# Three edits in two stages of a four-layer kernel: where the products of an attention layer are summed, where its sigmoid is written, and the place of one matrix product in a Fourier layer

## The chip, the cores and the metric

The kernel runs on one core of a Trainium2 chip. The time is the device time of one execution in microseconds (us), and lower is better. A NeuronCore has engines that run side by side, each with its own queue in program order: TensorE (PE, matrix products), VectorE (DVE), ScalarE (ACT), GpSimd (POOL, called Pool below) and the queues that issue DMAs (SP). They wait for each other by semaphores: a count that one engine raises and another waits for. SBUF is the on-chip memory of 128 partitions; PSUM is the small memory that TensorE writes its results to, which DVE and ACT can read and write too.

## The reference, cut to what matters

Four layers follow each other on an image of 2 x 64 channels (128 rows of the chip, one for each batch and channel) with 256 x 256 = 65,536 points; each adds its result to its input. The change touches the first and the third.

```python
# layer 0: attention over the nine neighbours of a point, two apart
un_em = _unfold3x3(em)
feature_score = jnp.einsum('bckhw,bchw->bkhw', un_em, em)
un_fea = _unfold3x3(inp)
comp_score = jax.nn.sigmoid(jnp.einsum('bckhw,c->bkhw', un_fea, w_comp))
phi = comp_score * feature_score
weighted_fea = jnp.einsum('bckhw,bkhw->bchw', un_fea, phi)
...
# layer 2: widen 64 channels to 384, filter 8 x 8 patches in frequency, 3 x 3 convolution, gate, project to 64
x = jnp.einsum('bchw,oc->bohw', x, w_in)
xf = jnp.fft.rfft2(xp) * fft_filter
xp = jnp.fft.irfft2(xf, s=(p, p))
x = lax.conv_general_dilated(x, w_dw, window_strides=(1, 1), padding=[(1, 1), (1, 1)], feature_group_count=C)
x1, x2 = jnp.split(x, 2, axis=1)
x = jax.nn.gelu(x1, approximate=False) * x2
return jnp.einsum('bchw,oc->bohw', x, w_out)
```

Before each layer the input is normalised by groups of channels. Layer 1 (two Mamba scans) and layer 3 (a cosine transform) are not touched.

## The kernel before

The stages run one after the other with a barrier between them: statistics and score maps, attention, Mamba, Fourier, cosine transform. In each stage every engine has its own program, and the order of the work is the order in which these programs are written; nothing is reordered by a planner.

**Attention** (`attention_layer`, from L366). The points are cut into 64 tiles of T = 1024 columns, and a step handles one tile; one short step more closes the stage, so there are 65. For tile s, TensorE multiplies the raw input `x` by a channel weight into `p_s` (`score`, L528: two halves of 512 columns). ACT takes the sigmoid of `p_s` into the SBUF buffer `sig` (L582), DVE forms `g` = (x - mean) * sig (`make_g`, L623) into a buffer with a margin, and ACT copies the margin from the tile before (L577). The nine neighbours are nine shifted reads of `g`: for k = 0 to 8 TensorE spreads the feature score of neighbour k to all channels in `p_f` (two PSUM buffers in turn, one bf16 product of two halves), and DVE multiplies it by the shifted `g` into `apr[k]` (L657). These nine products are summed in two places. Pool adds pairs of them in SBUF (L678, the list `PAIRS`: 0+1, 2+3, 4+5, 6+7, and 8 onto 6), and TensorE adds the four results into the PSUM tile `p_a` by products with the identity (`add`, in fp32; `SUMMED` tells how many of Pool's additions must be done). DVE then writes the output from `p_a` and the residual `xr` (`output`, L632) and takes its statistics (L645).

The order on TensorE in a step is: p_f 0, 1, 2, then the last addition of the step before (`add(s.other(-1), 6)`), p_f 3, 4, 5, the score of the next tile, p_f 6, add 0, p_f 7, add 2, p_f 8, add 4. All helpers run through `halves`, so every product of the stage has line L519. DVE's order is: products 0 to 4, output of the step before, products 5 and 6, its statistics, product 7, `make_g` of the next tile, product 8. With two p_f buffers, p_f k waits for product k-2.

**Fourier** (`fft_layer`, from L1378). A row r of 8 image lines is worked on in two slots, b = 0 and b = 1, one for each batch, 64 slots in all. In a slot TensorE runs through 24 ticks j (`slot`). The steps of the slot's own half: `conv` (one or two taps of the convolution as products into `p_c`, L1619), one at j = 1, 5, 9 and so on; these come first in a tick. `project` (L1627, L1629) multiplies the gated result of the slot before by the output weights, at j = 1 and j = 4. For the slot to come: `widen` (L1593) spreads a piece of the input over 384 channels into the single PSUM tile `p_fr`, at each odd j from 1 to 15; DVE multiplies it by the filter into `v` (`filter_`, L1853); `from_freq` (L1602) turns it back into `p_i` from j = 3 on, and ACT places it into `zb` (L1725). In slots b = 0 TensorE also turns the next row into frequencies (`turn`, L1572, and `to_freq`, L1582). Since `p_fr` is single, `widen` 1 waits until DVE has filtered `widen` 0's result.

DVE's program in a slot is 30 taps of the convolution (L1847, six units of five), with the filter for piece 0 after three taps, piece 1 after five, piece 2 after eight and so on (`FILTER_N`), and the additions of the residual (L1869) and the statistics (L1883) of the slot before at four places near the start. Pool adds ACT's taps (L1947) and multiplies for the gate (L1952, L1956).

Of the kernel before, what the change touches and what calls it, by code (L numbers as in the profile page):

```python
# [365 lines left out]
def attention_layer(nc, dram, fs, bn0, bn1, L, W, T):  # L366
# [11 lines left out]
    with ExitStack() as ctx:  # L378
        def sb(name, shape, dt=FP32):
            return ctx.enter_context(nc.sbuf_tensor(name, shape, dt))  # L380
# [11 lines left out]
        s_bias = sb("s_bias", [128, 1])  # L392
        x = [sb(f"ax{i}", [128, T]) for i in range(2)]
        xr = [sb(f"axr{i}", [128, T]) for i in range(2)]
        sig = [sb(f"sig{i}", [128, T]) for i in range(2)]
        g = [sb(f"g{i}", [128, GW]) for i in range(2)]
        fb = [sb(f"fb{i}", [96, T], BF16) for i in range(2)]
        pr = [sb(f"apr{i}", [128, T]) for i in range(NKS)]
# [24 lines left out]
        gnorm = GroupNorm(nc, ctx, "a", bn0, pair, p_a)  # L423
        block = ctx.enter_context(nc.Block())

        PAIRS = [(0, 1), (2, 3), (4, 5), (6, 7), (6, 8)]
        SUMMED = {0: 1, 2: 2, 4: 3, 6: 5}

        class Step:

# [83 lines left out]
        @block.tensor  # L514
        def _(pe):
            def halves(out, w, rhs, start=True, stop=True):
                for i in range(2):
                    c = slice(i * HALF, (i + 1) * HALF)
                    last = nc.tensor.matmul(out[:, c], w, rhs[:, c], start=start, stop=stop)  # L519
                return last  # L520

            pe.wait_ge(w_in, 48)
            gnorm.pe(pe)
            pe.wait_ge(gnorm.done, 1)
            nc.tensor.matmul(p_s[:, 0:1], comp[:, :], gnorm.gn[:, 6:7], start=True, stop=True).then_inc(bias_ps, 1)
            pe.wait_ge(ready, 1)

            def score(s):  # L528
                pe.wait_ge(x_in[s.par], s.pair * 16 + 16)
                if s.from_(1):  # L530
                    pe.wait_ge(sig_done, s.nth(0, 1) - 1)
                halves(p_s, comp_s[:, :], x[s.par]).then_inc(s_ps, 1)

            def add(s, k):
                pe.wait_ge(paired, s.nth(SUMMED[k] - 1, len(PAIRS)))
                if k == 0 and s.from_(1):
                    pe.wait_ge(xo_done, s.nth(0, 1) - 1)
                halves(p_a, ident, pr[k], start=(k == 0), stop=(k == 6)).then_inc(acc_done, 1)

            def step(s):  # L540
                pe.wait_ge(f_in[s.par], s.pair * 48 + 48)
                for k in range(NKS):
                    if s.from_(1) or k >= 2:
                        pe.wait_ge(prod_done, s.nth(k, NKS) - 2)
                    halves(p_f[(s.par + k) % 2], fsel[:, k, :], fb[s.par]).then_inc(f_ps, 1)
                    if k == 2 and s.from_(1):
                        add(s.other(-1), 6)
                    if k == 5 and not s.last and not s.other(1).last:
                        score(s.other(1))
                    if k >= 6:  # L550
                        add(s, 2 * (k - 6))

            score(Step(0, 0))
            run(step)(pe)
            add(Step(0, NK), 6)

        @block.scalar
        def _(act):
            act.wait_ge(w_in, 48)
            gnorm.act(act)  # L560
            act.wait_ge(ready, 1)

            def load_maps(s):
                if s.from_(2):
                    act.wait_ge(f_ps, s.nth(-1, NKS) - NKS)
                width = PAD if s.last else T
                for part in range(3):
                    act.dma_start(fb[s.par][32 * part:32 * part + 2 * NKS, 0:width],
                                  fs[part, :, bass.ds(s.at(T), width)]).then_inc(f_in[s.par], 16)

            def prepare(s):

                if s.from_(1):
                    act.wait_ge(g_done, s.nth(0, 1) - 1)
                    if s.from_(2):
                        act.wait_ge(prod_done, s.nth(-1, NKS) - NKS)
                    nc.scalar.activation(g[s.par][:, 0:2 * PAD], g[1 - s.par][:, T:T + 2 * PAD], ACT.Copy).then_inc(carried, 1)  # L577
                if not s.last:
                    act.wait_ge(s_ps, s.nth(0, 1))
                    if s.from_(2):  # L580
                        act.wait_ge(g_done, s.nth(0, 1) - 2)
                    nc.scalar.activation(sig[s.par][:, :], p_s[:, :], ACT.Sigmoid, bias=s_bias[:, :]).then_inc(sig_done, 1)  # L582

            def step(s):
                if not s.last:
                    load_maps(s.other(1))
                    prepare(s.other(1))

            load_maps(Step(0, 0))
            prepare(Step(0, 0))  # L590
            run(step)(act)

        @block.vector
        def _(dve):
# [20 lines left out]
            def make_g(s):  # L615
                if s.last:
                    dve.wait_ge(carried, NK)
                    nc.vector.memset(g[s.par][:, 2 * PAD:GW], 0.0).then_inc(g_done, 1)
                    return
                dve.wait_ge(sig_done, s.nth(0, 1))  # L620
                if s.from_(2):
                    dve.wait_ge(carried, s.nth(0, 1) - 1)
                nc.vector.scalar_tensor_tensor(out=g[s.par][:, 2 * PAD:GW], in0=x[s.par][:, :], scalar=mean_n[:, :],  # L623
                                               in1=sig[s.par][:, :], op0=ALU.add, op1=ALU.mult).then_inc(g_done, 1)

            def output(s):
                dve.wait_ge(acc_done, s.nth(3, 4))
                dve.wait_ge(xr_in[s.par], s.pair * 16 + 16)
                if s.from_(2):
                    dve.wait_ge(x_out[s.par], s.pair * 16)  # L630
                    dve.wait_ge(bn_done, s.nth(0, 1) - 1)
                nc.vector.scalar_tensor_tensor(out=xo[s.par][:, :], in0=p_a[:, :], scalar=rstd, in1=xr[s.par][:, :],  # L632
                                               op0=ALU.mult, op1=ALU.add).then_inc(xo_done, 1)
# [14 lines left out]
            def step(s):  # L648
                dve.wait_ge(g_done, s.nth(0, 1))
                if s.from_(1):  # L650
                    dve.wait_ge(carried, s.nth(0, 1) - 1)
                for k in range(NKS):
                    at = PAD + OFFS[k]
                    dve.wait_ge(f_ps, s.nth(k, NKS))
                    if s.from_(1) and k % 2 == 0 and k < 8:
                        dve.wait_ge(acc_done, s.nth(k // 2, 4) - 4)
                    nc.vector.tensor_tensor(out=pr[k][:, :], in0=g[s.par][:, at:at + T], in1=p_f[(s.par + k) % 2][:, :],  # L657
                                            op=ALU.mult).then_inc(prod_done, 1)
                    if k == OUT_K and s.from_(1):
                        output(s.other(-1))  # L660
                    if k == STAT_K and s.from_(1):
                        statistics(s.other(-1))
                    if k == G_K and not s.last:
                        make_g(s.other(1))
# [6 lines left out]
        @block.gpsimd  # L671
        def _(pool):
            def step(s):
                for n, (a, z) in enumerate(PAIRS):
                    pool.wait_ge(prod_done, s.nth(z, NKS))
                    if n == 4:
                        pool.wait_ge(paired, s.nth(3, 5))
                    nc.gpsimd.tensor_tensor(out=pr[a][:, :], in0=pr[a][:, :], in1=pr[z][:, :], op=ALU.add).then_inc(paired, 1)  # L678

            run(step)(pool)  # L680
# [697 lines left out]
def fft_layer(nc, dram, bn2, bn3, H, W):  # L1378
# [22 lines left out]
    with ExitStack() as ctx:  # L1401
# [158 lines left out]
        def _(pe):  # L1560
# [91 lines left out]
            def slot(r, b, s, first=False, no_next=False, no_row=False):  # L1652
                nb, ns = 1 - b, s + 1
                rows_left = not (isinstance(r, int) and r == NR - 1)
                for j in range(TICKS):
                    if j in CONV_AT:
                        conv(s, b, CONV_AT[j])
                    if not first and j in PROJECT_AT:
                        project(s - 1, nb, r if rows_left else None, PROJECT_AT.index(j))
                    if not no_next:  # L1660
                        if j in WIDEN_AT:
                            widen(ns, r + b, nb, WIDEN_AT[j])
                        if j in BACK_AT:
                            from_freq(ns, BACK_AT[j])
                        if j == NEXT_AT:
                            conv(ns, nb, 0)
                    if b == 0 and not no_row:
                        if j in TURN_AT:
                            turn(r + 1, TURN_AT[j])
                        if j in FREQ_AT:  # L1670
                            to_freq(r + 1, FREQ_AT[j])
# [665 lines left out]
```

## Time and profile before

| | us |
|---|---|
| runs of the kernel before, median of 3 | 20574.27 |
| lowest and highest of them | 20570.39, 20582.24 |
| the profiled execution, its own time | 20572.38 |
| its span | 20570.6 |
| attention stage, about | 1157 |
| Fourier stage, about | 3490 |

The profile comes from one execution. Its span is 1.8 us shorter than that execution's own time, and its time is 1.9 us below the median. TensorE's granted clock was 0.772 of full speed on average over the whole kernel: 0.89 in the attention stage and 0.96 in the Fourier stage. In a timeline row the first two numbers are the start and the time until the end of the row's last instruction, and the last bracket is the idle time of the engine ahead of it with the instruction that ended it.

### The profile page before, as it was taken

The numbers are of one execution on the slowest core, as the hardware profiler recorded it, in microseconds if no ns is written. First come the engines' busy times: TensorE is split into PE (matmuls) and PEld (weight loads), VectorE is DVE, ScalarE is ACT, GpSimd is POOL, SyncE is SP. The second block draws the span as 40 slices with busy tenths as digits, with TensorE's granted clock in tenths as the row PEclk, the third lists the DMA queues.
The fourth block names the chain that finished last, engine by engine and source line by source line (L and its number), as shares of the span: only waits on it lengthen the run. The fifth ranks groups of instructions, "written<-read, shape, count | busy, mean of one in ns | idle before, by whom it ended". The sixth has DMA issues, their size and how long they took to land. (4 is left out here: it accounts for less than half of the span.)

```text
span 20570.6 us, 184019 instructions
## 1 busy us (share of the span) xinstructions
PE 13872.1 (67%) x47074; PEld 5005.0 (24%) x47074; DVE 18437.9 (90%) x11898; ACT 11403.8 (55%) x12716; POOL 17177.7 (84%) x7352
## 2 busy tenths in 40 slices
PE   4885666666666666666666666666666668888885
PEld 2331111111111111111111111111111134444444
DVE  5778999999999999999999999999999979888896
ACT  1115555555555555555555555556555546666663
POOL 3777888888888888888888888888888868888891
PEclk8887777777777777777777777777777779999997
DMA  3224554555445554555445544555455511111113
GB/s 120 93 90 122 130 127 124 127 128 131 124 124 131 129 127 125 128 130 128 126 126 130 130 125 126 129 128 128 125 127 131 127 47 31 31 31 31 31 27 135
DMA packets 615483, 2240.63 MB, mean 109 GB/s; under 512 B 74881, under 2 KB 92147, under 8 KB 591091
## 3 DMA queue, kind: packets, MB, share of 16 engines
q1 hardware_dynamic: 610146, 2232.63, 42.0%
q10 hardware_dynamic: 5265, 7.14, 0.1%
q8 instruction: 33, 0.54, 0.0%
q14 instruction: 39, 0.32, 0.0%
HBM read 990.77 MB, written 174.96 MB: 57 GB/s over the span
## 5 line engine op out<-in xcount | busy, mean ns | idle before, releaser
L1358 POOL TENSOR_TENSOR h<-h,c_bc 128x1024 f32<-128x1024 f32 x4096 | 9597.4, 2358 | 1050.1 <-DVE h L1310 1036.5
L1310 DVE TENSOR_TENSOR_SCAN h<-da,state,px 128x1024 f32<-128x1024 f32 x3328 | 7810.9, 2347 | 524.0 <-PE py L1016 123.1
L1175 ACT ACTIVATE da<-d_bc,a_neg 128x1024 f32<-128x1024 f32 x3328 | 3811.8, 1145 | 3907.2 <-DVE h L1310 3882.4
L1002 PE MATMUL px<-cf,bsel 32*128 32x512 f32 x4096 | 2005.3, 1074 | 3605.7 <-DVE h L1310 3605.7
L1304 DVE TENSOR_TENSOR px<-px,du_bc 128x1024 f32<-128x1024 f32 x3328 | 4099.1, 1232 | 235.1 <-DMA du_bc<-du 46.2
L1947 POOL TENSOR_TENSOR acc<-acc,ta 128x1024 f32<-128x1024 f32 (+1 forms) x1040 | 2424.8, 2339 | 482.1 <-DVE acc L1847 344.0
L1016 PE MATMUL py<-h,ysel 128*32 128x512 f32 x16384 | 2370.4, 704 | 529.5 <-POOL h L1358 529.5
L1847 DVE SCALAR_TENSOR_TENSOR p_c<-zb,w_dw,p_c 128x1024 f32<-128x1024 f32 (+1 forms) x1560 | 1987.1, 1274 | 43.6 <-PE p_c L1619 11.1
L1310 DVE TENSOR_TENSOR_SCAN h<-px,state,xs 128x1024 f32<-128x1024 f32 x768 | 1772.7, 2338 | 274.6 <-ACT px L1175 272.3
L1350 POOL TENSOR_TENSOR xs<-du_bc,b_bc 128x1024 f32<-128x1024 f32 x768 | 1804.4, 2350 | 0.0
L1002 PEld LDWEIGHTS px<-cf,bsel 32*128 32x128 f32 x4096 | 488.6, 291 | 4714.0 <-DVE h L1310 4662.0
L1746 ACT ACTIVATE ta<-zb,w_dw 128x1024 f32<-128x1024 f32 (+1 forms) x1040 | 1169.0, 1129 | 317.2 <-POOL acc L1947 295.3
L1325 POOL TENSOR_TENSOR delta<-delta,sp 128x1024 f32<-128x1024 f32 x256 | 600.5, 2346 | 781.3 <-ACT sp L1127 781.3
L1602 PE MATMUL p_i<-basis,v 128*128 128x128 f32 x6144 | 967.2, 294 | 383.0 <-ACT zb L1725 373.1
L678 POOL TENSOR_TENSOR apr<-apr 128x1024 f32<-128x1024 f32 x325 | 824.1, 2543 | 383.0 <-DVE apr L657 377.5
L1619 PE MATMUL p_c<-zb,diag 128*128 128x512 f32 x2064 | 1007.4, 622 | 166.1 <-DVE acc L1847 131.3
L973 PE MATMUL pm<-hx,w_tap 128*128 128x512 f32 x1024 | 752.8, 902 | 534.5 <-ACT hx L1083 534.5
L1016 PEld LDWEIGHTS py<-h,ysel 128*32 128x32 f32 x16384 | 472.5, 121 | 2323.4 <-issue 1501.1
L944 PE MATMUL pm<-u,w_bc 128*64 128x512 f32 x1024 | 915.3, 1049 | 175.9 <-ACT sr L1099 175.9
L1602 PEld LDWEIGHTS p_i<-basis,v 128*128 128x128 f32 x6144 | 782.0, 194 | 812.8 <-ACT zb L1725 559.9
L657 DVE TENSOR_TENSOR apr<-g,p_f 128x1024 f32<-128x1024 f32 x585 | 690.3, 1215 | 253.5 <-PE p_f L519 252.1
L1725 ACT ACTIVATE zb<-p_i 128x384 f32<-128x384 f32 x1024 | 524.3, 512 | 633.0 <-PE p_i L1602 628.9
(222 smaller groups left out, 20340.6 us busy)
## 6 DMA issues: line engine op xcount, KB each, us to landing
d_bc<-delta SPq DMA_DIRECT2D x1024, 512.0 KB, 8.4
du_bc<-du SPq DMA_DIRECT2D x1024, 512.0 KB, 8.7
c_bc<-c_rows_dram SPq DMA_DIRECT2D x1024, 512.0 KB, 5.3
b_bc<-c_rows_dram SPq DMA_DIRECT2D x256, 512.0 KB, 8.0
hx<-x_dram SPq DMA_DIRECT2D x252, 256.5 KB, 6.0
st_x<-in_x_dram SPq DMA_DIRECT2D x32, 1024.0 KB, 4.9
ax<-in_x_dram SPq DMA_DIRECT2D x64, 512.0 KB, 3.4
xr<-x_dram SPq DMA_DIRECT2D x64, 512.0 KB, 5.9
```

The source lines that it names most:

```text
L1002: last = nc.tensor.matmul(px[(t.par + q + q // 2) % 2][:, cut], bsel[rows, q, :], cf[rows, cut], start=True, stop=True)
L1016: last = nc.tensor.matmul(py[32 * j:32 * j + 32, cut], ysel[:, :], h[:, (4 * q + j) % 8, cut], start=False, stop=(q == Q - 1))
L1175: nc.scalar.activation(out[:, :], d_bc[:, n % J, :], ACT.Exp, scale=a_neg[t.l][:, n:n + 1]).then_inc(da_done, 1)
L1304: nc.vector.tensor_tensor(out=x[:, :], in0=b[:, :], in1=du_bc[:, j, :], op=ALU.mult).then_inc(m1_done, 1)
L1310: nc.vector.tensor_tensor_scan(h[:, n % 8, PAD:T + PAD], a[:, :], x[:, :], state[:, 2 * t.l + t.b, n:n + 1], ALU.mult, ALU.add).then_inc(s ...
L1350: nc.gpsimd.tensor_tensor(out=xs[i][:, :], in0=du_bc[:, n % J, :], in1=b_bc[:, :], op=ALU.mult).then_inc(xs_done, 1)
L1358: nc.gpsimd.tensor_tensor(out=h[:, n % 8, 0:T], in0=h[:, n % 8, PAD:T + PAD], in1=c_bc[q % 2][:, :], op=ALU.mult).then_inc(m2_done, 1)
L1602: last = nc.tensor.matmul(p_i[:, c], v[j // 2 % 2][:, j % 2, c], basis[:, 1, :], start=True, stop=True)
L1619: last = nc.tensor.matmul(p_c[odd(s, u)][:, i * 512:i * 512 + rows * W], diag[:, oc, t, :], zb[b][:, oc, y:y + rows, dx:dx + W], start=(t ...
L1746: nc.scalar.activation(ta[odd(s, u)][t][:, 0:n * W].rearrange("p (y x) -> p y x", y=n), zb[b][:, oc, y:y + n, dx:dx + W], ACT.Identity, sc ...
L1847: nc.vector.scalar_tensor_tensor(out=out, in0=zb[b][:, oc, y:y + n, dx:dx + W], scalar=w_dw[:, oc, m:m + 1], in1=other, op0=ALU.mult, op1= ...
L1947: nc.gpsimd.tensor_tensor(out=acc[h][oc][:, c], in0=acc[h][oc][:, c], in1=ta[o][t][:, c], op=ALU.add).then_inc(added, 1)
```

## The change

In the attention stage Pool gets a sixth addition, 2 onto 0, third in its order, which waits for the second; TensorE's `add` of product pair 2 goes, so that three remain (0, 4 and 6). `add` 0 moves from behind p_f 6 to behind p_f 7 and waits for Pool's third addition; `add` 4 stays behind p_f 8 and waits for Pool's fourth. The counts that DVE waits for follow. The sigmoid is written over its own input in `p_s` and the two `sig` buffers go; `make_g` reads it from there, and `score` of the next tile waits until `make_g` has read it. In the Fourier stage `widen` stands ahead of `project` within a tick. The only tick that has both is j = 1, so only `widen` 0 and the first `project` of a slot change places.

```diff
-        sig = [sb(f"sig{i}", [128, T]) for i in range(2)]
...
-        PAIRS = [(0, 1), (2, 3), (4, 5), (6, 7), (6, 8)]
-        SUMMED = {0: 1, 2: 2, 4: 3, 6: 5}
+        PAIRS = [(0, 1), (2, 3), (0, 2), (4, 5), (6, 7), (6, 8)]
+        SUMMED = {0: 3, 4: 4, 6: 6}
+        NP, NA = len(PAIRS), len(SUMMED)
...
-                    pe.wait_ge(sig_done, s.nth(0, 1) - 1)
+                    pe.wait_ge(g_done, s.nth(0, 1) - 1)
...
-                    if k >= 6:
-                        add(s, 2 * (k - 6))
+                    if k == 7:
+                        add(s, 0)
+                    if k == 8:
+                        add(s, 4)
...
-                    if s.from_(2):
-                        act.wait_ge(g_done, s.nth(0, 1) - 2)
-                    nc.scalar.activation(sig[s.par][:, :], p_s[:, :], ACT.Sigmoid, bias=s_bias[:, :]).then_inc(sig_done, 1)
+                    nc.scalar.activation(p_s[:, :], p_s[:, :], ACT.Sigmoid, bias=s_bias[:, :]).then_inc(sig_done, 1)
...
-                                               in1=sig[s.par][:, :], op0=ALU.add, op1=ALU.mult).then_inc(g_done, 1)
+                                               in1=p_s[:, :], op0=ALU.add, op1=ALU.mult).then_inc(g_done, 1)
...
-                dve.wait_ge(acc_done, s.nth(3, 4))
+                dve.wait_ge(acc_done, s.nth(NA - 1, NA))
...
-                    if s.from_(1) and k % 2 == 0 and k < 8:
-                        dve.wait_ge(acc_done, s.nth(k // 2, 4) - 4)
+                    if s.from_(1) and k in SUMMED:
+                        dve.wait_ge(acc_done, s.nth(list(SUMMED).index(k), NA) - NA)
...
-                    if n == 4:
-                        pool.wait_ge(paired, s.nth(3, 5))
+                    if n in (2, NP - 1):
+                        pool.wait_ge(paired, s.nth(n - 1, NP))
...
+                    if not no_next and j in WIDEN_AT:
+                        widen(ns, r + b, nb, WIDEN_AT[j])
                     if not first and j in PROJECT_AT:
                         project(s - 1, nb, r if rows_left else None, PROJECT_AT.index(j))
                     if not no_next:
-                        if j in WIDEN_AT:
-                            widen(ns, r + b, nb, WIDEN_AT[j])
```

TensorE in the attention stage, one step from its p_f 5 on (`p_s` is the score of the next tile, `p_a<-apr0` is add 0). Before:

```order
L519 MATMUL p_f1<-fb0,fsel 128x512 x2
L519 MATMUL p_s<-ax1,comp_s 128x512 x2
L519 MATMUL p_f0<-fb0,fsel 128x512 x2
L519 MATMUL p_a<-apr0,a_mats 128x512 x2
L519 MATMUL p_f1<-fb0,fsel 128x512 x2
L519 MATMUL p_a<-apr2,a_mats 128x512 x2
L519 MATMUL p_f0<-fb0,fsel 128x512 x2
L519 MATMUL p_a<-apr4,a_mats 128x512 x2
```

The same stretch of TensorE after the change:

```order
L519 MATMUL p_f1<-fb0,fsel 128x512 x2
L519 MATMUL p_s<-ax1,comp_s 128x512 x2
L519 MATMUL p_f0<-fb0,fsel 128x512 x2
L519 MATMUL p_f1<-fb0,fsel 128x512 x2
L519 MATMUL p_a<-apr0,a_mats 128x512 x2
L519 MATMUL p_f0<-fb0,fsel 128x512 x2
L519 MATMUL p_a<-apr4,a_mats 128x512 x2
```

Add 0 has moved behind p_f 7 (the second `p_f1`), and the add of `apr2` is gone.

Pool in the attention stage, one whole step after the change (before, the third of these rows is not there):

```order
L678 TENSOR_TENSOR apr0<-apr0,apr1 128x1024 [waits product]
L678 TENSOR_TENSOR apr2<-apr2,apr3 128x1024 [waits product]
L678 TENSOR_TENSOR apr0<-apr0,apr2 128x1024 [waits products_paired,product]
L678 TENSOR_TENSOR apr4<-apr4,apr5 128x1024 [waits product]
L678 TENSOR_TENSOR apr6<-apr6,apr7 128x1024 [waits product]
L678 TENSOR_TENSOR apr6<-apr6,apr8 128x1024 [waits products_paired,product]
```

The new addition stands ahead of 4+5, 6+7 and 6+8, which all queue behind it.

TensorE in the Fourier stage, tick j = 1 of a slot, as one piece of the difference (`p_c` is conv, `p_qo<-ge` is project, `p_fr` is widen; ISA rows are waits):

```order
 L1619 MATMUL p_c1<-zb0,diag 128x512 x2
+L1588 ISA
+L1493 ISA
+L1593 MATMUL p_fr<-w_in,ft 128x384 x2
 L1641 ISA
 L1627 MATMUL p_qo<-ge00,w_out 64x512
...
 L1629 MATMUL p_qo<-ge11,w_out 64x512
-L1588 ISA
-L1493 ISA
-L1593 MATMUL p_fr<-w_in,ft 128x384 x2
```

Widen 0 stands directly behind conv now, and the four products of the first project follow it instead of leading it.

## Rows read from the trace of the kernel before

**Rows 1.** Busy time by stretch: start:end, length, then each engine; last granted clock, DMA.

```profile
392.00:1549.00 1157.00, 960.90 (x2454) 371.60 (x2454) 903.18 (x841) 138.16 (x127) 820.84 (x324) 0.89 0.28 92
16690.00:20180.00 3490.00, 2814.95 (x13806) 1505.57 (x13806) 3045.48 (x2731) 2142.26 (x2672) 3027.15 (x1300) 0.96 0.11 28
```

**Rows 2.** Waits in the attention stage: who for whom, us in total, times, longest.

```profile
DVE apr L657 <- PE p_f L519: 252.1, 144, 4.6
```

**Rows 3.** Timeline of DVE, one attention step at full clock (start, us, instructions).

```profile
913.73 2.35 DVE L657 TENSOR_TENSOR apr<-g,p_f 128x1024 f32<-128x1024 f32 x2 [3.76 <-PE p_f L519]
...
920.64 1.20 DVE L657 TENSOR_TENSOR apr<-g,p_f 128x1024 f32<-128x1024 f32 x1
921.76 1.28 DVE L623 SCALAR_TENSOR_TENSOR g<-ax,mean_n,sig 128x1024 f32<-128x1024 f32 x1
...
930.22 1.22 DVE L657 TENSOR_TENSOR apr<-g,p_f 128x1024 f32<-128x1024 f32 x1 [2.39 <-PE p_f L519]
```

**Rows 4.** Timeline of TensorE, the same step and the end of the one before.

```profile
909.87 3.38 PE L519 MATMUL p_a<-apr,a_mats 128*128 128x512 f32 x4 [1.51 <-POOL apr L678]
...
919.75 1.88 PE L519 MATMUL p_a<-apr,a_mats 128*128 128x512 f32 x4
921.47 0.60 PE L519 MATMUL p_f<-fb,fsel 96*128 96x512 bf16 x2
921.90 1.88 PE L519 MATMUL p_a<-apr,a_mats 128*128 128x512 f32 x4
...
927.76 1.98 PE L519 MATMUL p_a<-apr,a_mats 128*128 128x512 f32 x4 [1.54 <-POOL apr L678]
```

**Rows 5.** Timeline of Pool, the same step.

```profile
915.02 2.36 POOL L678 TENSOR_TENSOR apr<-apr 128x1024 f32<-128x1024 f32 x1 [2.91 <-DVE apr L657]
...
921.93 8.08 POOL L678 TENSOR_TENSOR apr<-apr 128x1024 f32<-128x1024 f32 x3 [1.08 <-DVE apr L657]
```

**Rows 6.** All instructions of two lines: count, min/median/max ns, first and last start.

```profile
L678 POOL TENSOR_TENSOR apr<-apr x325: 2331/2356/3350, 394.7 to 1550.0; 128x1024 f32<-128x1024 f32 x163
L623 DVE SCALAR_TENSOR_TENSOR g<-ax,mean_n,sig x64: 1277/1279/1284, 391.0 to 1511.7; 128x1024 f32<-128x1024 f32 x64
```

**Rows 7.** Waits in the Fourier stage, columns as in Rows 2.

```profile
DVE v L1853 <- PE p_fr L1593: 355.8, 256, 21.1
...
PE p_fr L1593 <- DVE v L1853: 73.7, 63, 2.3
...
POOL acc L1947 <- POOL ge L1956: 22.4, 93, 0.2
```

**Rows 8.** Timeline of TensorE around j = 1 of a slot b = 1.

```profile
18069.61 1.99 PE L1619 MATMUL p_c<-zb,diag 128*128 128x512 f32 x4
18071.52 1.08 PE L1627 MATMUL p_qo<-ge,w_out 128*64 128x512 f32 x4
...
18073.54 0.92 PE L1593 MATMUL p_fr<-w_in,ft 64*128 64x384 f32 x4
18075.61 0.92 PE L1593 MATMUL p_fr<-w_in,ft 64*128 64x384 f32 x4 [1.16 <-DVE v L1853]
```

**Rows 9.** Timeline of DVE in that slot: filter 0, the first residual addition, filter 2.

```profile
18074.60 0.96 DVE L1853 TENSOR_TENSOR v<-p_fr,filt 128x768 f32<-128x768 f32 x1 [1.26 <-PE p_fr L1593]
...
18076.66 0.68 DVE L1869 TENSOR_TENSOR fxo<-p_qo,fxr 128x512 f32<-128x512 f32 x1
...
18084.77 0.96 DVE L1853 TENSOR_TENSOR v<-p_fr,filt 128x768 f32<-128x768 f32 x1 [0.34 <-PE p_fr L1593]
```

**Rows 10.** Timeline of a slot b = 0: TensorE's conv at j = 1.

```profile
18011.57 3.78 PE L1619 MATMUL p_c<-zb,diag 128*128 128x512 f32 x4 [3.74 <-DVE acc L1847]
```

**Rows 11.** DVE's filter 0 of the same slot.

```profile
18019.14 0.96 DVE L1853 TENSOR_TENSOR v<-p_fr,filt 128x768 f32<-128x768 f32 x1 [3.78 <-PE p_fr L1593]
```

**Rows 12.** Timeline of Pool, late in that slot b = 1.

```profile
18105.03 4.88 POOL L1947 TENSOR_TENSOR acc<-acc,ta 128x1024 f32<-128x1024 f32 x2 [1.52 <-DVE acc L1847]
```

**Rows 13.** ACT's normalisation of a row in the Fourier stage: all of them.

```profile
L1707 ACT ACTIVATE hn<-raw,f_gn x31: 2077/2079/2082, 16751.5 to 19904.9; 128x2048 f32<-128x2048 f32 x31
```

## The prediction, as it was put on record

> **What bounds the kernel now.** I read the busy time by stretch first [rows 1]. The change lies in two of the stages. The attention stage takes about 1157 us of the span, the Fourier stage about 3490. In neither is an engine full: DVE, the busiest, works 903 of 1157 us and 3045 of 3490 us. So each stage is held by a chain that runs from engine to engine, and the question is which links of it the edits shorten. The views that show this are the waits and then the timelines.
>
> In the attention stage DVE loses 252.1 us, all of it to TensorE's p_f [rows 2]. The timeline of a step shows where. Product 3 starts at 913.73 and product 3 of the next step at 930.22: a step is 16.49 us here [rows 3]. Most of DVE's idle time is the 2.39 us ahead of product 3. That product needs p_f 3, which stands behind the last addition of the step before on TensorE, and this addition waited 1.54 us for Pool until 927.76 [rows 4]. Pool was late because its addition 6+7 can start only after product 7 (end 920.64 + 1.20 = 921.84, start 921.93), and 6+8 follows [rows 3, 5]. The loop is therefore: product 3, DVE's work up to product 7, Pool's 6+7 and 6+8, TensorE's add 6 and p_f 3, product 3.
>
> Two things lengthen it. First, Pool's three additions from 921.93 take 8.08 us, where a lone one takes 2.36; 8.08 - 2 x 2.36 = 3.36, which is the longest addition of the stage, 3.350 us against a median of 2.356 [rows 5, 6]. It is 6+7, and it starts while DVE's `make_g` runs (921.76 to 923.04). `make_g` is DVE's only operation in the step whose two large inputs both lie in SBUF; the addition that runs from 915.02 to 917.38 takes its normal 2.36 us beside products and the output, which read one input from PSUM [rows 3, 5]. Second, the clock: add 6 took 1.98 us at 927.76 and 3.38 us at 909.87, one at the level of 2.4 GHz and the other mostly at 1.2 GHz [rows 4]. The 64 `make_g` run from 391.0 to 1511.7 us, so a mean step is 1120.7 / 63 = 17.8 us, 1.3 us above the step at full clock [rows 6]. The granted clock of the stage is 0.89 [rows 1].
>
> In the Fourier stage DVE waits 355.8 us for p_fr [rows 7]. In a slot b = 1, TensorE runs conv (1.99 us), both parts of the first project (18071.52 to 18073.54) and only then widen 0 [rows 8]. DVE waited 1.26 us for it [rows 9]. And since p_fr is single, TensorE then stood idle 1.16 us until DVE had filtered it [rows 8]. That idle time comes once in nearly every slot: 73.7 us in 63 cases, 1.17 each [rows 7].
>
> **The change, part by part: attention.** I take the time from the start of product 3.
> (1) The sigmoid in PSUM. `make_g` now has one input in PSUM, like the output and the products, so I let 6+7 take its 2.36 us: 1.0 us less on the loop. ACT's sigmoid is not on the loop, and `make_g`'s own time (1.28 us) I leave. The new wait of the score for `make_g` costs nothing, since the products of the same `g` run before it in any case.
> (2) The sixth addition. Pool's first addition of the loop, 2+3, starts 915.02 - 913.73 = 1.29 us in [rows 3, 5]. Behind it come 0+2, 4+5, 6+7 and 6+8. Products 5 and 7 end at 4.7 and 8.1 us, before Pool gets to them, so the five run one behind another: 5 x 2.36 = 11.8 us, done at 13.1 us. Pool pays up to 0.24 us where it waits for its own result (22.4 / 93 in the Fourier stage [rows 7]), twice here: 13.1 to 13.6. The three additions of 8.08 us hold one such wait and no visible gap, so I take 13.2. Before, 6+8 ended at 921.93 + 8.08 - 2.36 = 927.65, that is 13.92 us in. Pool's own chain has become the bound in place of product 7, and of the 1.0 us saved only 0.3 to 0.8 arrives. Pool's total, 6 x 2.36 = 14.2 us, fits in the step.
> (3) From the end of 6+8 to product 3 it took 930.22 - 927.65 = 2.57 us [rows 3, 5], which stays. A step at full clock becomes 13.2 + 2.57 = 15.8 us, with 15.7 and 16.2 as ends.
> (4) The removed add is 1.72 us of TensorE (919.75 to 921.47 [rows 4]). At full clock it hides beside DVE. Add 0 now waits for 0+2, done at 1.29 + 2 x 2.36 = 6.0 us, and holds up p_f 8, which DVE wants only at 9.2 us; add 0 of 1.9 us ends at 8. At half clock it matters more: before, p_f 7 and p_f 8 each stood behind an add that takes twice as long, now only p_f 8 does.
> (5) The clock. Half clock costs 1.3 us a step now. TensorE's long idle stretch around p_f 2 shrinks with (1) from 1.54 us ahead of add 6 to about 0.7; a new idle of about 0.8 us opens ahead of add 0. No row shows the granted clock of this pattern. From below the cost is 0, from above the present 1.3; I take 0.25, since the stretch with least work, ahead of add 6, is the one that gets shorter, and half clock reaches fewer links of the loop.
> Sum: 15.8 + 0.25 = 16.05 us against 17.8, 1.75 us x 64 steps = 112 us. Ends: 17.8 - 15.7 = 2.1 us, 134 us; 17.8 - (15.9 + 1.3) = 0.6 us, 38 us.
>
> The Trainium skill says in SBUF — State Buffer, Who interferes with whom, that a DVE instruction with two SBUF inputs contends with a GpSimd instruction that reads SBUF, and one with at most one SBUF input does not. The trace agrees with both halves, by the 3.35 us and the 2.36 us of (1). The page's Practical consequences add that the one which issues later blocks fully; by that, had the sigmoid stayed in SBUF beside six additions, `make_g` could have been the one to wait. It changes no term above.
>
> **Fourier.** Widen 0 now follows conv directly. Its own 0.92 us moves ahead of project, so p_fr comes some 2 us earlier, and DVE's 1.26 us in a slot b = 1 goes. TensorE does the same work in another order: DVE filters while project runs, and when project ends widen 1 can start at once, so the 1.16 us of idle goes too. What is late next: filter 2 waits for the chain of TensorE (0.34 us before [rows 9]); DVE arrives 1.26 us earlier and TensorE 1.16 us, so the gain of the slot is the smaller, 1.16 us. In slots b = 0 conv at j = 1 often runs at half clock (3.78 against 1.99 us [rows 8, 10]), and DVE waited 3.78 us for filter 0 [rows 11]. Of that some 2 us go, but DVE waits for TensorE again at the next filters, so the chain of TensorE decides, with 1.16 us again. The first residual addition needs project, which ends 0.92 us later than now, at about 18074.5; DVE, with its 1.26 us gone, comes to it at 18075.4 [rows 8, 9]: hidden, by 0.9 us. Pool waits 1.52 us for DVE late in slot b = 1 [rows 12], more than the 1.16 us by which DVE comes earlier, so Pool does not become the bound. 62 slots have both a widen and a project: 62 x 1.16 = 72 us. Ends: 60 where Pool or a second wait takes some back; 90 where half clock strikes less. A row of two slots takes (19904.9 - 16751.5) / 30 = 105.1 us now [rows 13] and should take 102.8.
>
> **The rivals.** (A) Half clock in the attention stage costs as much as now: 38 + 72 = 110 us, 20462 us. For it: TensorE's work per step falls and with it its share. Against: its longest idle stretch shortens. (B) The sigmoid in PSUM does not free Pool, so 6+7 stays at 3.35 us: the step is 17.05 us, 48 + 72 = 120 us, 20452 us. Against it speaks the addition beside the output at 2.36 us. (C) The Fourier gain is given back, because Pool or ACT's placing takes the chain over: 112 us, 20460 us. For it: Pool is busy 3027 of 3490 us [rows 1]. Against: its 1.52 us of wait. (D) Slower: TensorE stays at 1.2 GHz for nearly all of the attention stage. Its work in a step, nine p_f of 0.43 us (921.47 to 921.90) and four fp32 products of 1.72 us [rows 4], is 10.8 us at full clock and 21.5 at half; with half a microsecond for the loop's waits, 22 us, which is 4.2 us x 64 = 269 us more, less 72: 20769 us. It decides from a step of 17.8 + 72 / 64 = 18.9 us on. Against: at half clock TensorE is never idle, and in the rows it came back to full clock between 909.87 and 919.75 us [rows 4].
>
> The Trainium skill, TensorE: Matmul & The Clock Gate, What's actually happening, states that activity releases the throttle and the default is the slow clock. By that rule, taking matmuls out of the step argues for A and D.
>
> **How the numbers follow.** Forecast 0.69; A 0.14; B 0.06; C 0.07; D 0.04. The forecast is 112 + 72 = 184 us off the profiled execution's 20572.4: 20388, and as the median of the runs is 1.9 us higher, 20390. The forecast's own ends are 134 + 90 = 224 us, 20350, and 60 + 60 = 120 us, 20454; A to C end at 20464. A range of 20350 to 20470 holds all but D and some tails. Within 0.2%, 41 us, is what a measurement can hardly tell from none. Faster by more than that holds in all cases but D: 0.94. Same 0.02, slower 0.04.
>
> **What would show it.** In the profile after: no Pool addition above 2.4 us in L678, 390 of them; product 3 to product 3 at 15.8 us where the clock is full; a mean spacing of `make_g` near 16.05 us; the granted clock of the stage at or above 0.89. In the Fourier stage TensorE's waits for DVE's v fall from 63 to a few, and L1707 comes every 102.8 us. It is wrong if additions still take 3.3 us (B), if steps scatter as widely as now (A), or if Pool's waits for DVE vanish while the row's time stays (C).

## The result: 1.5% slower, and the loss lies in a stage that no edit touches

The changed kernel takes 20888.71 us (median of 4 runs, 20859.31 to 20902.15) against 20578.26 us before (4 runs beside them). The ratio is 1.0149, with a 95% interval of 1.0132 to 1.0167. The forecast was 20390 us with a range up to 20470.

The page of the profile after, its first line and its DMA queues (packets, MB, share of 16 engines' time):

```profile
span 20888.0 us, 183503 instructions
...
q14 instruction: 340, 2.78, 0.0%
```

The same two lines before:

```profile
span 20570.6 us, 184019 instructions
...
q14 instruction: 39, 0.32, 0.0%
```

The queue that brings instructions to the engines moved 301 packets more, though the program has become a little shorter. The next three views give each stage a row of before and of after; the first and last start of one line's instructions measure its length. First the attention stage of after, Pool's additions and DVE's `make_g` (count, min/median/max ns, first and last start), which answer to [rows 6]:

```profile
L678 POOL TENSOR_TENSOR apr<-apr x390: 2338/2356/2377, 394.7 to 1439.2; 128x1024 f32<-128x1024 f32 x195
L623 DVE SCALAR_TENSOR_TENSOR g<-ax,mean_n,p_s x64: 1272/1274/1280, 391.0 to 1401.4; 128x1024 f32<-128x1024 f32 x64
```

No addition takes more than 2.38 us, and a mean step is (1401.4 - 391.0) / 63 = 16.04 us, against 17.8. The stage ends 1550.0 - 1439.2 = 110.8 us earlier.

Then the Fourier stage, ACT's row normalisation over the whole stage, before and after (the row of before in [rows 13] begins with the second of the 32):

```profile
L1707 ACT ACTIVATE hn<-raw,f_gn x32: 2077/2079/2092, 16677.6 to 19904.9; 128x2048 f32<-128x2048 f32 x32
```

```profile
L1707 ACT ACTIVATE hn<-raw,f_gn x32: 2077/2080/2094, 17081.1 to 20228.7; 128x2048 f32<-128x2048 f32 x32
```

3227.3 us became 3147.6: 79.7 us gained. Last the Mamba stage, which lies between the two and which no edit touches, by Pool's 4096 products of its scan, before and after:

```profile
L1358 POOL TENSOR_TENSOR h<-h,c_bc x4096: 2328/2353/2463, 1623.5 to 16620.0; 128x1024 f32<-128x1024 f32 x196
```

```profile
L1358 POOL TENSOR_TENSOR h<-h,c_bc x4096: 2329/2354/2450, 1510.3 to 17023.4; 128x1024 f32<-128x1024 f32 x196
```

14996.5 us became 15513.1, 516.6 us more, with instructions that take as long as before. The sum is -110.8 + 516.6 - 79.7 = +326 us, against 317 us of span; the other 9 us lie outside these rows.

What grew is idle time of DVE. Its waits in the Mamba stage of after (who for whom, us in total, times, longest):

```profile
DVE h L1310 <- ACT px L1175: 290.9, 418, 2.0
DVE px L1304 <- issue: 274.2, 60, 10.1
DVE h L1310 <- issue: 221.5, 55, 5.5
DVE h L1310 <- DVE px L1304: 141.4, 570, 0.5
```

The two "issue" rows are new; before, DVE has no such row for these lines. Issue is time in which an engine waits for nothing that the profile shows. They come in pairs, 495.7 us in 115 stops. One pair on DVE's timeline of after:

```profile
3061.69 2.35 DVE L1310 TENSOR_TENSOR_SCAN h<-da,state,px 128x1024 f32<-128x1024 f32 x1
3067.17 1.23 DVE L1304 TENSOR_TENSOR px<-px,du_bc 128x1024 f32<-128x1024 f32 x1 [3.13 <-issue]
3072.65 2.35 DVE L1310 TENSOR_TENSOR_SCAN h<-da,state,px 128x1024 f32<-128x1024 f32 x1 [4.25 <-issue]
```

The instructions of DVE's queue around it tell where in the program it is. L829 is the line of the Mamba loop (a hardware loop of 61 rounds whose body is 325 instructions on DVE); the first two rows below are line L829 in the stretch 3060 to 3070, the third L1305 in 3066 to 3073, columns as for L1707:

```profile
L829 DVEq COMPARE_BRANCH  x1: 63/63/63, 3061.8 to 3061.8; - x1
L829 DVEq FUSED_REGOPS  x1: 63/63/63, 3066.8 to 3066.8; - x1
...
L1305 DVEq FUSED_REGOPS  x1: 46/46/46, 3072.3 to 3072.3; - x1
```

The branch at the loop's end runs at 3061.8 and the loop's first instruction at 3066.8, 5.0 us later (this pair is on the short side; the median of the 60 jumps back is 6.1 us). The fourth, the product at 3067.17, starts; the fifth (L1305), which waits for nothing, comes 5.1 us after it. In the kernel before, the same branch and first instruction are 0.3 us apart (2905.6 and 2905.9). So DVE stops for want of instructions, when it jumps back and again four instructions on.

Counted in DVE's program as built, the loop starts at instruction 709 after the change and at 715 before: the attention stage lost six DVE instructions, because the wait of product 2 for `add` 2 is gone wherever a step is written out. The second stop lies between 712 and 713. **The theory** (P in the expectations) is that instructions come in blocks, that a block begins at 713, and that before the change the loop began two instructions behind that boundary, by luck. The Trainium skill, Runtime: NRT & Kernel Launch, Instruction fetch mechanics, describes this: blocks of 256 instructions, room for two of them in most engines, and a taken branch whose target is not among the two has to fetch it first. By that rule a loop of 325 instructions is free of stops where it covers two blocks and refetches in every round where it covers three. **The rival** (Q) is that the stops come from something else that changed: the programs of Pool or TensorE, which shifted too, or what the new schedule does to memory traffic or clock.

### The profile page after: what moved, and what is told of

The parts are those of the page before. It is cut to its first block and busy times, and to the rows that moved or that the text cites. A ratio compares the mean times of both kernels' runs of the same rounds, so it can differ in the third digit from the quotient of the medians.

```text
span 20888.0 us, 183503 instructions
## 1 busy us (share of the span) xinstructions
PE 13701.7 (66%) x46814; PEld 4924.9 (24%) x46814; DVE 18437.5 (88%) x11898; ACT 11408.4 (55%) x12716; POOL 17271.3 (83%) x7417
## 5 line engine op out<-in xcount | busy, mean ns | idle before, releaser
L678 POOL TENSOR_TENSOR apr<-apr 128x1024 f32<-128x1024 f32 x390 | 913.6, 2356 | 182.9 <-DVE apr L657 174.4
L1175 ACT ACTIVATE px<-d_bc,a_neg 128x1024 f32<-128x1024 f32 x768 | 834.9, 1108 | 13.6 <-DVE h L1310 13.6
```

Source lines behind the costliest of these rows:

```text
L1175: nc.scalar.activation(out[:, :], d_bc[:, n % J, :], ACT.Exp, scale=a_neg[t.l][:, n:n + 1]).then_inc(da_done, 1)
```

## Experiments

### Does moving the loop, and only that, remove or make the stops?

Two kernels are the changed one with idle DVE instructions ahead of the attention steps; each holds two waits on a count that was reached long ago. A third is the kernel before with 250 of them, and a fourth has the Fourier edit alone.

```diff
             rstd = gnorm.gn[:, 5:6]
+            for _ in range(8):          # two waits share an instruction: 4 more; 6 gives 3 more, 500 gives 250
+                dve.wait_ge(w_in, 48)
```

> The changed kernel with four idle DVE instructions (each two waits that are already met) ahead of the attention steps, so that DVE's Mamba loop starts at its instruction 713 instead of 709; in the kernel before it was 715. Theory P (placement): in the trace after the change DVE stops twice in every round of the Mamba loop, about 5 us each, once between the loop's last branch and its first instruction and once between instructions 712 and 713, 115 stops with 496 us of idle put down to issue; if a boundary of instruction fetch lies at 713, a loop of 325 instructions that starts there needs one piece less. Expected 20375 to 20395 us, no stops, and the Mamba stage back at its 14996 us. Rival Q (not placement: something that the new schedule, Pool's or TensorE's program, or memory traffic does to the Mamba stage): four idle instructions change nothing, 20870 to 20900 us.

> The same with three idle instructions: the loop starts at 712, one instruction ahead of the supposed boundary. Theory P: the stops stay, 20860 to 20900 us, and the second stop of a round comes directly behind the loop's first instruction and so lies in front of the first product. Rival Q: no difference from the changed kernel and none from four more instructions. If the boundary lies elsewhere than read from the trace, this one is fast as well.

> The kernel before with 250 idle DVE instructions ahead of the attention steps and nothing of the change: DVE's Mamba loop starts at 965, which is 709 plus 256. Theory P, with pieces of 256 instructions as the Trainium skill's runtime page has them: 20574 + 496 to 517 us for the stops and about 10 to 20 us for the idle instructions themselves, 21080 to 21115 us, and the stops at the same two places of the loop as in the changed kernel. Rival Q: 20585 to 20600 us.

> The kernel before with only the Fourier edit (first widening ahead of the first output product); DVE's instructions stay where they were. Theory P: the gain of the Fourier stage alone, 72 to 80 us, so 20494 to 20502 us, and a Mamba stage without stops. Rival Q, if the Fourier edit had a part in the loss: over 20574 us.

Measured beside a kernel before of 20587.71 us (7 runs); the first row is the result above, beside 20578.26. "Mamba stage" is first to last start of Pool's 4096 products, "stops" is DVE's idle time put down to issue ahead of its products and scans there:

| kernel | loop starts at | time, us | ratio, 95% interval | Mamba stage, us | stops, us |
|---|---|---|---|---|---|
| changed | 709 | 20888.71 | 1.0149 (1.0132 to 1.0167) | 15513.1 | 495.7 |
| changed, 4 more | 713 | 20367.02 | 0.9894 (0.9878 to 0.9911) | 14995.9 | none |
| changed, 3 more | 712 | 20954.58 | 1.0180 (1.0163 to 1.0197) | 15591.7 | 577.0 |
| before, 250 more | 965 | 21077.32 | 1.0240 (1.0223 to 1.0257) | 15475.1 | 470.0 |
| before, Fourier edit | 715 | 20482.37 | 0.9950 (0.9934 to 0.9967) | 14994.4 | none |

One idle instruction is worth 588 us: with three the loop starts one instruction ahead of the boundary and pays, with four it starts on it and does not. The queue of instructions goes with it, in the pages of the kernels with four and with three more:

```profile
span 20365.0 us, 183507 instructions
...
q14 instruction: 39, 0.32, 0.0%
```

```profile
span 20963.2 us, 183506 instructions
...
q14 instruction: 339, 2.78, 0.0%
```

With three more, both stops lie ahead of the round's first product, as expected, so nothing runs beside the second; in the changed kernel the product (1.23 us) did. That makes 577.0 / 60 = 9.6 us of idle time a round against 495.7 / 60 = 8.3, and the time lies 55 us above the range that I gave; with four more it lies 8 us under its range. DVE's timeline of that kernel:

```profile
3059.37 2.35 DVE L1312 TENSOR_TENSOR_SCAN h<-da,state,px 128x1024 f32<-128x1024 f32 x1
3070.54 1.23 DVE L1306 TENSOR_TENSOR px<-px,du_bc 128x1024 f32<-128x1024 f32 x1 [8.82 <-issue]
```

The kernel before with 250 idle instructions has nothing of the change and pays all the same: its loop starts 256 instructions behind the changed kernel's. That excludes Pool's and TensorE's programs and the new schedule. Its time lies 3 us under the range that I gave. The Fourier edit alone lies 12 us under its range. It gains 105 us against the median of the runs beside it; those scatter by 23 us, and their median is 15 us above the profiled execution of before. Against that execution (20572.38) it gains 90 us, and L1707 shows 80 of them: 16676.5 to 19823.4 us, 3146.9 against 3227.3. Part of the rest lies in this stage too. By the same two starts, the profiled kernels without the Fourier edit take 3227.3 to 3245.2 us for it and those with the edit 3146.6 to 3148.9, so what the edit gains depends on which kernel it is held against: 80 to 98 us.

### How far does the good place reach?

If two blocks of 256 are the room, the loop of 325 instructions may start up to 187 instructions behind a boundary, at 713 + 187 = 900, and no further.

```diff
+            for _ in range(370):        # 185 more; 372 gives 186 more
+                dve.wait_ge(w_in, 48)
```

> The kernel before with 185 idle DVE instructions: the Mamba loop of 325 instructions takes up 900 to 1224. With boundaries at 713 and every 256 instructions behind it (969, 1225), that is the last place at which the loop still lies in two pieces. Theory P with a window of two pieces: no stops, 20585 to 20600 us (the idle instructions cost some us). Rival (it matters how close behind the start the next boundary lies, or that a boundary lies ahead of it, not how many pieces the loop covers): stops in each round as in the changed kernel, over 20800 us.

> One idle instruction more: the loop takes up 901 to 1225, and its last instruction, the branch, lies in a third piece. Theory P: one or two stops of some 5 us in each of 61 rounds, 300 to 580 us over the run with 185, so 20890 to 21180 us. Rival: the same time as the run with 185.

With 185 more: 20619.70 us, 1.0014 (1.0003 to 1.0026) of a kernel before of 20591.32, with no stop. With 186 more: 20956.30 us, 1.0179 (1.0149 to 1.0208). In the second, DVE's waits in the Mamba stage begin with

```profile
DVE px L1306 <- issue: 357.6, 60, 9.2
```

The loop's last instruction alone lies in the third block, and 337 us follow (2 runs against 8). A round has one stop here, 6.0 us on average ahead of the product, behind the jump back; the Mamba stage grew from 15010.7 to 15369.8 us. So the count of blocks that the loop covers decides, as the rule has it; how the stops spread over a round depends on where the boundaries cut it. The instruction queue moved 341 packets with 186 more, as many as with two stops a round (340), and 41 with 185 more: it tells whether the loop is fetched again, and not what that costs. The run with 185 more lies 28 us above the kernel before beside it, more than the 11 to 26 us I allowed. Not all of it is the idle instructions. In the trace, Pool's first Mamba product comes 17 us later (1640.3 against 1623.5), about 0.09 us for each, and the Mamba stage itself is 14 us longer (15010.7 against 14996.5), which no run explains.

### What are the parts of the change worth, with the loop in a good place?

Four kernels: the attention edits without the Fourier edit; the sigmoid in PSUM alone (with the waits that go with it); the sixth addition alone, so the change's `PAIRS`, `SUMMED` and places of `add`, with the sigmoid in SBUF; and the sigmoid with the Fourier edit. Where the sixth addition is in, four idle instructions keep the loop at 713; the others have it at 715. The edit of the second, in short:

```diff
-                    nc.scalar.activation(sig[s.par][:, :], p_s[:, :], ACT.Sigmoid, bias=s_bias[:, :]).then_inc(sig_done, 1)
+                    nc.scalar.activation(p_s[:, :], p_s[:, :], ACT.Sigmoid, bias=s_bias[:, :]).then_inc(sig_done, 1)
...
-                                               in1=sig[s.par][:, :], op0=ALU.add, op1=ALU.mult).then_inc(g_done, 1)
+                                               in1=p_s[:, :], op0=ALU.add, op1=ALU.mult).then_inc(g_done, 1)
```

> The attention edits without the Fourier edit, with the four idle DVE instructions that keep the Mamba loop on one boundary. If the parts add up: 112 us off the attention stage and nothing elsewhere, 20455 to 20465 us against a kernel before of 20574. If the two parts of the change disturb each other, it differs from that by more than 15 us.

> The kernel before with the sigmoid written over its input in PSUM and nothing else; five additions on Pool, four on TensorE; DVE's Mamba loop stays at 715. Theory of the prediction: the addition 6+7 falls from 3.35 to 2.36 us, so a step at full clock falls from 16.49 to 15.5 us (6+8 done at 8.20 + 2 x 2.36 = 12.9 us, and 2.57 us to product 3). The clock decides the rest: at its present cost of 1.3 us a step the mean is 16.8 us and the gain 62 us, 20510 us; if the shorter idle stretch ahead of add 6 lets the clock stay up, 16.0 us and 113 us, 20460 us. Rival (the port has no part in it): 6+7 stays at 3.35 us and the time at 20574 us.

> The kernel before with the sixth addition on Pool in place of one of TensorE's, the sigmoid still in SBUF, and the four idle DVE instructions. If a DVE instruction and a Pool addition with all inputs in SBUF shut each other out: Pool's chain of five additions, already the bound, takes 1.0 us more, or DVE's g waits for Pool; a step at full clock is 16.7 to 17.0 us against 16.49, but half clock reaches fewer links, so a mean of 17.0 to 17.8 us and 20520 to 20574 us. If g and the additions did not meet here, 16.1 us and 20460 us.

> The sigmoid in PSUM and the Fourier edit, without the sixth addition: 92 us below the run with the sigmoid alone if they add up. Is it under 20367 us, the sixth addition costs more than it brings; I expect 20370 to 20420 us, so that the sixth addition is worth 0 to 50 us, all by the clock.

Beside a kernel before of 20587.56 us (13 runs); the last two columns are from each trace, a mean step by the 64 starts of `make_g` and a step at full clock by a pair of product 3:

| kernel | time, us | ratio, 95% interval | mean step | at full clock |
|---|---|---|---|---|
| before | 20587.56 | | 17.8 | 16.49 |
| attention edits | 20475.60 | 0.9948 (0.9932 to 0.9965) | 16.03 | 15.67 |
| sigmoid alone | 20468.47 | 0.9945 (0.9928 to 0.9961) | 16.10 | 15.52 |
| sixth addition alone | 20537.47 | 0.9977 (0.9968 to 0.9987) | 17.03 | 16.65 |
| sigmoid and Fourier | 20382.91 | 0.9903 (0.9886 to 0.9919) | 16.21 | |
| all edits, 4 more (above) | 20367.02 | 0.9894 (0.9878 to 0.9911) | 16.04 | 15.67 |

The sigmoid alone brings nearly all of the attention gain. Its rows, Pool's additions and `make_g`, answer to [rows 6]:

```profile
L675 POOL TENSOR_TENSOR apr<-apr x325: 2339/2360/2370, 396.1 to 1443.8; 128x1024 f32<-128x1024 f32 x163
L620 DVE SCALAR_TENSOR_TENSOR g<-ax,mean_n,p_s x64: 1273/1274/1281, 392.4 to 1406.7; 128x1024 f32<-128x1024 f32 x64
```

The longest addition fell from 3.350 to 2.370 us, with no other edit in the kernel: the addition was slow because `make_g` beside it read both inputs from SBUF, as argued. With the sixth addition and the sigmoid in SBUF, the addition 6+7 took 3.34 us (median of 65) and the step at full clock 16.65 us: there the port costs its 1.0 us in full, since Pool's chain is the bound. `make_g` itself waits too in that kernel, since it now meets a Pool addition that started first:

```profile
L628 DVE SCALAR_TENSOR_TENSOR g<-ax,mean_n,sig x64: 1285/1451/2103, 392.3 to 1464.9; 128x1024 f32<-128x1024 f32 x64
```

Its median is 1.451 us against 1.279 [rows 6], its longest 2.103.

Of the four expectations, three hold: the sigmoid alone came out 8 us above the lower of its two values, the sixth addition alone inside its range (with 16.65 us for the step, just under the 16.7 to 17.0), the sigmoid with the Fourier edit inside its own. The attention edits lie 11 us above their range, but that was set against a kernel before of 20574; against the 20587.56 beside them they gain the forecast 112 us.

What the sixth addition adds is small: 20382.91 against 20367.02, 16 us (from two sets of runs), and 7 us the other way between the attention edits and the sigmoid alone, which is within their scatter. At full clock it makes the step longer (15.67 against 15.52 us), because Pool's five additions in a row are later than product 7. It pays that back in what half clock costs. The same stretch, 400 to 1430 us, in the trace of the sigmoid alone and then of the changed kernel (start:end, length, PE, PEld, DVE, ACT, POOL busy, granted clock, DMA):

```profile
400.00:1430.00 1030.00, 886.79 (x2419) 343.46 (x2418) 884.32 (x825) 135.40 (x126) 751.09 (x319) 0.96 0.32 101
```

```profile
400.00:1430.00 1030.00, 799.12 (x2172) 293.26 (x2170) 890.31 (x828) 135.41 (x126) 898.46 (x384) 0.95 0.32 101
```

The clock is no higher with the sixth addition; what falls is what half clock costs, from 16.10 - 15.52 = 0.58 us a step to 0.37. Steps with the sigmoid alone are either 15.5 or 17.2 us, those of the changed kernel 15.67 or 16.6 to 16.7 us. A long step thus loses 1.0 us in place of 1.7, and DVE's waits show why. The product of DVE that is held up in a long step, with the sigmoid alone, in the changed kernel, and with the sixth addition alone:

```profile
866.38 2.35 DVE L654 TENSOR_TENSOR apr<-g,p_f 128x1024 f32<-128x1024 f32 x2 [3.10 <-PE p_f L518]
```

```profile
919.72 1.22 DVE L657 TENSOR_TENSOR apr<-g,p_f 128x1024 f32<-128x1024 f32 x1 [0.97 <-PE p_f L519]
```

```profile
825.77 2.35 DVE L662 TENSOR_TENSOR apr<-g,p_f 128x1024 f32<-128x1024 f32 x2 [3.84 <-PE p_f L520]
```

The first and the third are product 3, behind add 6; the second is product 8, behind add 0. Of 60 steps with the sigmoid alone 23 are long, and in all of them DVE waits 2.9 to 3.1 us ahead of product 3, against 1.4 in a step at full clock. Of 60 in the changed kernel 26 are long; there that wait stays at 0.59 us and product 8 waits 0.5 to 1.0. So what counts is which add the stretch at 1.2 GHz meets. It is not the smaller number of fp32 products on TensorE: the sixth addition alone has as few, and its long steps take 18.3 us against 16.65, 1.65 more. Why the stretch meets add 0 in one kernel and add 6 in another was not isolated.

## Why the prediction was wrong, point by point

**What bounds the kernel.** Right for both stages, as far as they go. The Mamba stage, 15,000 of 20,570 us, was not looked at, since no edit lies in it. That is the step that failed: the sum took it for granted that untouched code costs what it cost. The missing term is +517 us, larger than all others together, and the list of what would make the prediction wrong has nothing like it. Rival D ended on the slow side by the clock of the attention stage and had no part in it: the clock of the stage rose.

**Attention (1), the port.** Right. 6+7 fell from 3.35 to 2.36 us, in the changed kernel and with the sigmoid alone.

**(2) and (3), Pool's chain as the new bound.** Right. In the changed kernel 6+8 is done 13.16 us into the step (13.2 was taken) and the step at full clock is 15.67 us (15.8). Pool shows the chain as one row of four or more additions with no gap, here 2+3 to 6+7:

```profile
910.74 9.41 POOL L678 TENSOR_TENSOR apr<-apr 128x1024 f32<-128x1024 f32 x4 [1.18 <-DVE apr L657]
921.10 2.35 POOL L678 TENSOR_TENSOR apr<-apr 128x1024 f32<-128x1024 f32 x1 [0.96 <-DVE apr L657]
```

The second row, 6+8, waited 0.96 us for product 8. It did so in a step at half clock, in which add 0 took 3.34 us and held up p_f 8 (DVE's product 8 starts at 919.72 after 0.97 us of idle, and it waits so in every long step): the hold-up that point (4) saw hidden at full clock is what half clock costs now.

**(5), the clock.** 0.25 us a step was taken; it is 16.04 - 15.67 = 0.37. The granted clock of the stage went from 0.89 [rows 1] to 0.95.

**Sum of the attention stage.** 112 us forecast, 111 measured. The low ends of the working do not fit together: (3) has 16.2 us as the slow end of a step at full clock, the sum takes 15.9; and the sum's low end is 38 us, where the range takes 60 without deriving it. Neither bears on the outcome.

**Fourier.** 72 us forecast with ends of 60 and 90; 80 measured against the profiled kernel before, up to 98 against other kernels without the edit. The idle time of TensorE ahead of widen 1 is gone, as its waits of after show:

```profile
PEld p_fr L1593 <- DVE v L1853: 37.7, 44, 2.8
...
PE p_fr L1593 <- DVE v L1853: 2.2, 1, 2.2
```

One wait of PE is left of 63 [rows 7]; the same wait of the weight load (PEld) fell from 112.5 to 37.7 us. At j = 1 of a slot b = 1 of after:

```profile
18438.68 1.99 PE L1619 MATMUL p_c<-zb,diag 128*128 128x512 f32 x4
18440.59 0.92 PE L1593 MATMUL p_fr<-w_in,ft 64*128 64x384 f32 x4
18441.44 1.08 PE L1627 MATMUL p_qo<-ge,w_out 128*64 128x512 f32 x4
18442.45 1.08 PE L1629 MATMUL p_qo<-ge,w_out 64*64 64x512 f32 x4
18443.45 0.92 PE L1593 MATMUL p_fr<-w_in,ft 64*128 64x384 f32 x4
```

Widen 1 follows project at once, where it came 1.16 us late [rows 8]. DVE's filter 0 of that slot runs at 18442.31 without idle time, and filter 2 waits 0.39 us where 0.44 was worked out (0.34 + 1.26 - 1.16). A row of two slots takes (20228.7 - 17153.8) / 30 = 102.5 us, where 102.8 was expected. The 8 us above the forecast are near the end that I gave to half clock striking less, but no run isolates them.

**The rivals.** A, B and C fell: the clock costs less than before, the port is free, the Fourier gain arrived. Of the terms that the sum had, none was mis-sized by more than 8 us against the profiled kernel before; with the loop moved by four instructions the changed kernel takes 20367 us, 23 us from the forecast and inside its range. That kernel is also the fastest that was run, 1.06% under the kernel before (0.9878 to 0.9911) and 2.5% under the change as it was made.

## What to carry to other kernels

A hardware loop that is longer than one block of instructions and shorter than two has good and bad places (measured here for one of 325 on DVE; for other lengths and engines it is the arithmetic of the blocks, not a measurement), and an edit in any earlier stage, even one that takes instructions away, moves it. Count each engine's instructions ahead of its long loops in both programs, and where the count changes, treat the place as a term of the sum with a price on both sides; a profile shows the bad place as idle time put down to issue just behind the loop's branch, and as packets on the instruction queue. To compare two schedules, bring the loops to the same place first, with idle instructions if need be.

## What the runs showed of the hardware

- For a DVE loop of 325 instructions, starts at 713, 715 and 900 are free of stops, and starts at 709, 712, 901 and 965 cost 337 to 588 us in 61 rounds. The boundaries lie at 713 and at 969 and 1225, counted from the start of DVE's own program; where the first one falls was read off a stop and could not be worked out from the program.
- From the loop's branch to its first instruction DVE takes 0.32 us where there is no stop (60 jumps of the kernel before). With stops the median of 60 jumps is 6.1 us at 709, 6.5 at 712, 5.9 at 965 and 7.5 at 901, and single ones take 3.4 to 12.0. The second stop has a median of 4.8, 5.0 and 4.7 us at 709, 712 and 965; at 901 there is none. Part of a jump passes beside DVE's last scan (2.35 us), so the idle time is less: 8.3, 9.6, 7.8 and, at 901, 6.0 us a round. Why the jump takes longest at 901 is not shown.
- A DVE instruction with both inputs in SBUF delays a Pool addition that starts beside it by 1.0 us (3.350 against 2.356 us); with one input moved to PSUM the delay is gone and the DVE instruction takes the same time (1.279 and 1.274 us). Where the Pool addition started first, it was the DVE instruction that took longer, 1.451 us.
